# Identity products in TensorE's waits: an eight-layer attention and feed-forward kernel on one core

## What is computed

```python
x = x + L0_xattn(ctx, norm(x))   # causal attention of the 56 tokens over the first 56 context rows
x = x + L0_ffn(norm(x))          # 8 experts, top 2 by softmax gates, gelu
x = x + L1_xattn(norm(x), ctx)   # self attention, cross attention over 1500 keys, two linear maps, three layer norms
x = x + L1_ffn(norm(x))          # gated unit with 4 bit weights and 16 bit activations, five maxima over all of x
x = x + L2_xattn(norm(x), ctx)   # 16 heads of 64, softmax over 1500 keys, output map, layer norm
x = x + L2_ffn(norm(x))          # 64 small units of 16
x = x + L3_xattn(norm(x), ctx)   # 16 heads of 8, masked softmax over 1500 keys
x = x + L3_ffn(norm(x))          # 8 experts, top 2, a layer norm behind each expert
```

## Time and profile before

| | us |
|---|---|
| median of 3 runs | 1704.77 |
| lowest and highest | 1703.37, 1705.45 |
| the profiled execution's own time | 1701.17 |
| its span, first to last instruction | 1699.1 |
| TensorE busy, matmul | 1484.5 |
| VectorE busy | 1248.8 |
| mean granted clock of TensorE | 0.942 |

### The profile page before, as it was taken

One profiled execution on the slowest core, in us unless ns is written; L12 is line 12 of the kernel. 1 busy time (PEld: TensorE's weight loads), 2 busy tenths in 40 slices (PEclk: granted clock), 3 DMA queues, 4 the chain that ended last, 5 costly groups with the idle time before them and its releaser, 6 DMA issues. The chain is left out here.

```text
span 1699.1 us, 39660 instructions
## 1 busy us (share of the span) xinstructions
PE 1484.5 (87%) x15231; PEld 1254.6 (74%) x15231; DVE 1248.8 (74%) x2582; ACT 840.8 (49%) x1266; POOL 331.9 (20%) x447
## 2 busy tenths in 40 slices
PE   3897387447899999999999999969999999996995
PEld 2897255336799999999999998437777777774895
DVE  4312664794788888888888887558888888884698
ACT  1342133133666666666666665245656666552432
POOL 0110000001333333333333330031111110100320
PEclk9899699667999999999999999989999999998998
DMA  1455067100211111111111100045456455531010
GB/s 36 116 168 122 21 158 172 37 1 1 73 37 38 37 36 36 36 36 38 55 44 44 36 0 0 7 105 141 110 122 148 112 129 131 122 85 51 26 38 23
DMA packets 93021, 115.95 MB, mean 68 GB/s; under 512 B 12152, under 2 KB 78248, under 8 KB 92904
## 3 DMA queue, kind: packets, MB, share of 16 engines
q1 hardware_dynamic: 92904, 114.25, 26.3%
HBM read 76.42 MB, written 0.46 MB: 45 GB/s over the span
## 5 line engine op out<-in xcount | busy, mean ns | idle before, releaser
L1643 ACT CAST l2att_PT<-PS 125x512 fp32r<-125x512 f32 x336 | 175.3, 595 | 221.3 <-PE PS L1582 221.3
L2377 DVE TENSOR_REDUCE l3att_parts<-PS 112x1 f32<-112x500 f32 x384 | 245.6, 669 | 50.3 <-PE PS L2115 42.7
L1683 DVE TENSOR_REDUCE l2att_neg<-PS 128x1 f32<-128x1500 f32 x112 | 192.7, 1720 | 77.4 <-PE PS L1575 77.4
L1689 DVE TENSOR_TENSOR l2att_PT<-PS,l2att_PT 125x512 fp32r<-125x512 f32 x336 | 210.1, 681 | 1.5 <-ACT l2att_PT L1643 1.5
L2244 ACT ACTIVATE l3att_P<-PS 125x1344 f32<-125x1344 f32 x128 | 165.2, 1291 | 77.2 <-PE PS L2136 77.2
L1582 PEld LDWEIGHTS PS<-all_ident,l_P 128*125 128x125 f32 x1344 | 163.6, 187 | 14.9 <-DVE l_P L1697 6.3
L1652 ACT ACTIVATE l_P<-PS,l2att_neg 128x1500 f32<-128x1500 f32 x112 | 171.0, 1527 | 3.9 <-DVE l2att_neg L1683 3.9
L1614 PE MATMUL PS<-l2att_PT,l_cc 125*128 125x256 f32 x576 | 170.5, 296 | 0.0
L1582 PE MATMUL PS<-all_ident,l_P 128*125 128x128 f32 x1344 | 165.4, 273 | 4.8 <-DVE l_P L1697 4.8
L1616 PE MATMUL PS<-l2att_PT,l_cc 125*128 125x256 f32 x576 | 162.5, 282 | 0.0
L1618 PE MATMUL PS<-l2att_PT,l_cc 125*128 125x256 f32 x576 | 162.4, 282 | 0.0
(11 more groups left out here) (549 smaller groups left out, 2860.5 us busy)
## 6 DMA issues: line engine op xcount, KB each, us to landing
l3att_KS<-l3att_kh SPq DMA_DIRECT2D x128, 187.5 KB, 4.0
l_cT<-in_ctxT SPq DMA_DIRECT2D x18, 750.0 KB, 6.5
l_c<-in_ctx SPq DMA_DIRECT2D x16, 750.0 KB
l3att_cT<-in_ctxT SPq DMA_DIRECT2D x16, 750.0 KB, 4.4
l3att_KS<-l3att_kl SPq DMA_DIRECT2D x64, 187.5 KB, 4.4
l_QP<-in_ctx SPq DMA_DIRECT2D x10, 672.0 KB
l_QP<-in_ctxT SPq DMA_DIRECT2D x8, 750.0 KB, 7.1
l0f_w<-in_L_ffn_W SPq DMA_DIRECT2D x16, 256.0 KB, 3.1
```

The lines of the kernel that those rows point to most:

```text
L1643: act.copy(PT[:, 4 * g:4 * g + 4, PLACE[u1], 0, :], PS[0:CHUNK, 3 * s1 + g, :].rearrange("k (c r) -> k c r", r=128)).then_inc(hi_in, 1)
L1683: v.tensor_reduce(neg[:, s:s + 1], E, XY_AXES, ALU.max, negate=True).then_inc(top_in, 1)
L1689: v.tensor_tensor(PT[:, 4 * g:4 * g + 4, at, 1, :], PS[0:CHUNK, 3 * s1 + g, :].rearrange("k (c r) -> k c r", r=128), PT[:, 4 * g:4 * g + 4 ...
L2377: v.tensor_reduce(parts[:, u % 2, half, i:i + 1], PS[0:HROWS, PLACES[p], 0:BANK_KEYS], X_AXIS, ALU.max, negate=True).then_inc(top_in, 1)
```

## The change

A helper `keep_busy(pe, bank, count)` multiplies the 128 x 128 identity by itself `count` times into a given bank, whose content nothing uses. Each product is two weight loads and two matmuls. It is called 18 times in one execution, 474 products in all, unrolled: in `l0a` 5, 14 and 30; in `l0f` 28; in `l1s` 30, 14, 52 and 44; in `l1c` 40 and 46; in `l1q` 20, 30, 18 and 14; in `l2fold` 30; in `l2m` 22; in `l3att` 7; in `l3f` 30. The counts are fixed. The products wait for nothing, and the next real instruction of TensorE stands behind them in its list. In `l1q` the wait for `b_in` also moves ahead of `spread(OQ)`, since the bank that it guards is now written earlier.

```diff
@@ -132,6 +132,11 @@
 
+    def keep_busy(self, pe, bank, count):
+
+        for _ in range(count):
+            pe.matmul(self.PS[:, bank, 0:128], self.ident[:, :], self.ident[:, :], start=True, stop=True)
+
     def sb(self, ctx, name, shape, dt=F32):
@@ -291,9 +296,12 @@
             def _(pe):
+                self.keep_busy(pe, 6, 30 if self_keys else 5)
                 pe.wait_ge(w_in, 80 if self_keys else 32)
...
                           start=True, stop=True).then_inc(fold_ps, 1)
+                if not self_keys:
+                    self.keep_busy(pe, 6, 14)
                 for k in range(2):
@@ -315,9 +323,11 @@
                 if self_keys:
+                    self.keep_busy(pe, 7, 14)
                     pe.wait_ge(cnt_in, 1)
...
                               stop=True).then_inc(len_ps, 1)
+                self.keep_busy(pe, 7, 52 if self_keys else 30)
                 pe.wait_ge(p_done, 1)
@@ -335,6 +345,8 @@
                     mm.then_inc(z_ps, 1)
+                if self_keys:
+                    self.keep_busy(pe, 7, 44)
 
@@ -496,6 +508,7 @@
             def _(pe):
+                self.keep_busy(pe, 6, 30 if final else 28)
                 pe.wait_ge(w_in, 16 * SETUP_DMAS)
@@ -878,6 +891,7 @@
                     mm.then_inc(z_ps, 1)
+                self.keep_busy(pe, 0, 40)
                 pe.wait_ge(n2_ready, 1)
@@ -893,6 +907,7 @@
                     mm.then_inc(y_ps, 1)
+                self.keep_busy(pe, 2, 46)
 
@@ -1159,9 +1174,11 @@
                     if i == 3:
+                        self.keep_busy(pe, 6, 20)
                         spread(GQ)
...
                 products("wvT", "wo", 0, ORDER[0:2])
+                self.keep_busy(pe, 6, 30)
                 spread(UQ)
@@ -1177,8 +1194,10 @@
                 mm.then_inc(cb_ps, 1)
+                pe.wait_ge(b_in, 8)
+                self.keep_busy(pe, ORDER[2], 18)
                 spread(OQ)
-                pe.wait_ge(b_in, 8)
+                self.keep_busy(pe, ORDER[2], 14)
                 for k in range(2):
@@ -1387,6 +1406,7 @@
             def _(pe):
+                self.keep_busy(pe, 0, 30)
                 for k in range(2):
@@ -1817,6 +1837,7 @@
                 outputs(1)
+                self.keep_busy(pe, 3, 22)
 
@@ -2061,6 +2082,7 @@
                     mm.then_inc(xt_ps, 1)
+                self.keep_busy(pe, 0, 7)
                 pe.wait_ge(w_in, 16)
```

## The result

The kernel after takes 1695.06 us in the median of 14 executions (1691.83 to 1699.46), that of before 1703.78 in the median of 14 (1698.98 to 1710.29). The ratio is 0.9948, with a 95% interval of 0.9938 to 0.9959: about 8.9 us won. Forecast were 12.1, a time of 1692.7 and a range of 1685 to 1702. The profiled execution took 1695.17 with a span of 1693.1.

A forecast was written before the change was run, and what follows sets the result against it. TensorE was taken to lose time at half clock (about 197 us of the span) in short stages behind waits. The steps' terms summed to −12.1 us, from 1704.77 to 1692.7 us, with a range of 1685 to 1702.

The forecast's parts named there:

- Steps 1 to 3, 5 and 6: Runs in `l0a` (−2.0, −1.5), `l0f` (−2.5), and `l1s` behind its head (−1.7, −1.2 us): faster work behind waits.
- Step 7: `l1c`, 40 products in a 10.6 us wait: transposes and products behind at full clock, −2.5 us (−2 to −3).
- Step 4: `l1s` head, 30 products overrunning their wait: 0 if the clock holds, +1.6 us if it falls, taken as +0.8.
- The clock rule: Anywhere on TensorE: clock holds over gaps of 2 us or less, even chance at 2.5, more likely lost at nearly 3.
- Step 8: `l1q`, 20 products before `spread(GQ)`, where there is no wait: paid in full, +4.4 us.
- the rival that called it absorbed: The 20 before `l1q`'s gate-maximum spread cost 0, total 1688.3 us; chance 0.08.
- Step 10: `l1q`, 18 before and 14 behind `spread(OQ)`: +0.4 us overrun, −2.3 from output products at full clock.
- Step 11: `l2fold` head, 30 products: 1 us over the wait, or 2.6, against 3 won behind; −1.5 us (−2.2 to 0).
- Step 12: `l2m` 22 and `l3att` 7: six key products at full clock, 2.7 instead of 5.37 us; −1.5 us (0 to −2.2).
- Step 13: `l3f`, 30 products in an 8.4 us wait, VectorE's gate steps stretched beside GpSimd's biases: −1.0 us (0 to −2.2).
- That the clock doesn't rise for these products: All runs: products mostly of zeros leave the clock at half, runs overrun by 57 us, 1761 or more; chance 0.05.
- Half of the wins stop at another engine: Whole kernel: ScalarE's copies, GpSimd or transfers set the end, half the wins remain, 1701.5 us; chance 0.15.

The follow-up runs named there:

- e6_half: The kernel after with every run at half its length: 1701.44 us, ratio 0.9988 to before.
- e9_shift: `e7_best` without the 18 before `l1q`'s third spread and with 14 products added at the end of `l3att`: 1689.95 us, ratio 0.9932 to before.
- e2_only20: The kernel before plus only the 20 products in front of the spread of the gate maximum in `l1q`: ratio 1.0024, 4.1 us slower.
- e10_best_plus20: `e7_best` with the 20 products before the spread of the gate maximum put back: 1692.54 us, ratio 0.9939 to before.
- e8_clear: `e7_best` also without the 18 and 14 in `l1q`, the 22 in `l2m` and the 7 in `l3att`: 1691.44 us, ratio 0.9935 to before.
- e1_no20: The kernel after without the 20 products in front of the spread of the gate maximum in `l1q`: 1692.09 us, ratio 0.9944 to before.
- e7_best: After without `l1q`'s 20 and 30, `l1c`'s 46, the 30 at `l1s`'s head and in `l3f`, with 25 in `l2fold`: 1688.83 us, ratio 0.9915 to before.
- e11_best_plus_l3f: `e7_best` with the 30 products at the head of `l3f` put back: 1686.44 us, ratio 0.9905 to before.
- e12_best_plus_l1s: `e7_best` with the 30 products at the head of `l1s` put back: 1688.83 us, ratio 0.9917 to before.

## Why the prediction was right, and what it mis-sized

What each stage took against before, mean over profiles with the runs less mean over those without (12 changed kernels, `e6_half` left out, and `e9_shift` in the row of steps 9 and 10; `l1q` ends and `l2fold` begins with the change of block, and only three of the seven in the row of steps 9 and 10 have the 30):

| Steps | Forecast, us | Profiles with, without | With less without, us |
|---|---|---|---|
| 1, 2 (`l0a`) | −3.5 | 10, 2 | −3.5 |
| 3 (`l0f`) | −2.5 | 10, 2 | −3.2 (with: −4.3 to −1.9) |
| 4 (`l1s` head) | +0.8 | 5, 7 | +1.1 (0.2 or 1.4 to 1.9) |
| 5, 6 | −2.9 | 10, 2 | −2.4 |
| 7 (`l1c`, 40) | −2.5 | 10, 2 | −1.8 |
| 8 (the 20) | +4.4 | 4, 8 | +4.1 |
| 9, 10 (`l1q`, 30, 18, 14) | −1.9 | 7, 4 | −1.0 (with: −2.3 to −1.2) |
| 11 (`l2fold`) | −1.5 | 10, 2 | −0.5 (with: −3.4 to +1.0) |
| 12 (`l2m`, `l3att`) | −1.5 | 9, 3 | −0.7 |
| 13 (`l3f`) | −1.0 | 5, 7 | −0.3 |

The right column sums to −8.2 us, against 8.9 measured and 12.1 forecast. Single entries are good to about 1 us, and least sure where only two or three profiles are without. The mechanism held and the sizes were too hopeful: steps 7 and 10 to 13 each miss 0.7 to 1.0 us, and step 3 gave 0.7 more. The range took that in.

**Steps 1 to 3, 5 and 6 hold.** Between VectorE's, ScalarE's and TensorE's turns a faster TensorE turn is time won. The price of 0.222 us held: 5.61 − 1.14 = 4.47 us of wait for 20 products are 0.224 each. Step 7 gave 2.2 us against before in nine of the ten profiles, within its bounds, and 0.7 in that of after, in which the clock was at half again from 299.0 to 302.4 us.

**Step 4 holds in both its cases.** "0 or +1.6" were measured as about 0.2 and 1.4 to 1.9. The clock rule behind it was too sharp: gaps of 2.90 us fell out both ways, and so did the 2.1 us from which the rule was made. Timeline, PE, the twelve transposes behind such a gap in `l1c`, of before and then of after:

```profile
286.05 1.57 PE L848 MATMUL PS<-all_ident,l_P 128*125 128x128 f32 x12 [2.10 <-ACT l_P L920]
```

```profile
274.66 2.55 PE L861 MATMUL PS<-all_ident,l_P 128*125 128x128 f32 x12 [2.09 <-ACT l_P L935]
```

In before the clock stayed up, in after it was at half from 275.1 to 281.9.

**Step 8 holds**, shown by `e2_only20` and by `e10_best_plus20`: a run that stands in no wait is paid in full, and by the rival that called it absorbed `e2_only20` would have had ratio 1.0000.

**Step 10 was mis-sized.** The output products became faster just as said: 2.39 us won in all seven profiles with the 18 and 14, where 2.3 were forecast. But the four without any run in `l1q` also scatter there, from 1.1 won to 0.6 lost, since the clock fell at other moments. And the 18 delay the maximum behind `spread(OQ)`, by 0.05 us in after and 0.7 to 1.25 in the other six, 0.9 in the mean, where I had taken 0.4; in `e8_clear` and `e9_shift`, without them, the delay is 0.0. The 30 of step 9 cost nothing, as forecast: from before `spread(UQ)` to behind `spread(OQ)` `e1_no20`, which has the 30 and the 18, lost 1.24 us, and `e7_best`, which has the 18 alone, 1.12.

**Step 11 was mis-sized** in what stands against its overrun. The run reaches past its wait as priced. Against before, the first token copy of `l2fold` came 0.6 us later behind the block's start in after, 2.0 to 2.2 in the three others with 30 products, where the clock fell, 1.0 to 1.1 in four of the six with 25, and 0.5 earlier in `e8_clear` and `e9_shift`, whose 25 ran at full clock (5.82 us). But what the products behind it give back is 1.5 us (with less without), not 3.

**Step 12 was mis-sized.** The key products are faster, 2.0 us at the third chunk, but 1.2 to 4.0 go again in the head of the loop. Timeline, PE, of after, at the place where the clock fell:

```profile
1132.71 0.48 PE L2137 MATMUL PS<-l3att_KS,l3att_QB 97*112 97x500 f32 x1 [0.20 <-DVE l3att_parts L2399]
1133.36 0.48 PE L2137 MATMUL PS<-l3att_KS,l3att_QB 97*112 97x500 f32 x1 [0.17 <-DVE l3att_kl L2363]
1134.62 0.69 PE L2137 MATMUL PS<-l3att_KS,l3att_QB 97*112 97x500 f32 x2 [0.78 <-DVE l3att_parts L2399]
1135.97 0.54 PE L2168 MATMUL PS<-all_ident,l3att_negs 112*3 112x112 f32 x2 [0.67 <-DVE l3att_negs L2432]
```

No gap is longer than 0.78 us, and the clock is at half from 1135.3. My rule looked at single gaps of 2 us and more, and here none stands. Nor do the short ones settle it: in before the same gaps of 0.78 and 0.68 us stand at this place, and the clock stayed up. It fell near there in the profiles with the 22 and 7 and also in the three without, while before happened to stay up. So this is no price of the two runs; that before stayed up there was luck.

**Step 13 was mis-sized**, by GpSimd's additions as shown under `e11_best_plus_l3f`: 2.5 to 2.7 us won from the block's start to the gate values in four of five profiles (0.5 in `e11_best_plus_l3f`), and 3.3 to 3.7 lost behind them in the same four up to the next additions, of which the stretched steps explain some 2; the seven without it lost 1.2 in the mean further on, so that the ends differ by 0.3.

**The rivals.** That the clock doesn't rise for these products is out (0.975, and 0.977 with transposes). That it falls again in each rest is out for these counts, and is what happened at half of them in `l0a`. "Half of the wins stop at another engine" came true in step 13 alone; what steps 10 to 12 miss went to runs that overran and to the clock.

**Left open.** The loop of `l1c`, which holds no runs, took from 5.0 us less to 1.7 more than before in changed kernels. Where the clock falls there differs from profile to profile; why at that moment, no run tells. `e1_no20`'s missing 1 to 3 us are followed in one profile of each kernel only; whether its other executions lost them at the same places isn't shown.

## What to carry to other kernels

A short stage in which engines take turns behind a wait is worth keeping the clock up for, and the run must reach nearly to the end of its wait: at half the length the whole set won 0.1%, which is not clear of nothing. Before each run, look for the engine that is idle because of TensorE at that place; where there is one, as before the spread of the gate maximum, each product of 0.222 us is paid in full. Where the clock may fall just before the run, count its products at 0.42 us: the 25 and 30 of `l2fold` overran their wait in most profiles and gave back part of what step 10 had won. A win of some us that is made early stays, but one that brings two engines together on the same memory, or moves a stage a little, is easily given back, so judge such runs by on-and-off pairs over several executions and not by one profile.

## What the hardware showed unexpectedly

- The clock fell in a stretch whose longest TensorE gap was 0.78 us, and behind the same gap it fell in one profile and held in another: 2.90 us (after, `e12_best_plus_l1s`), 2.48 (`e7_best`, `e8_clear`) and 2.1 (after, before).
- Transposes of the identity held the clock up as well as products: 0.977 against 0.975.
- A VectorE step of 0.22 us on two inputs took 2.16 and 2.06 us beside GpSimd's additions of 2.36 and 2.38, ending 0.07 to 0.08 after them.
- TensorE's "issue" gaps, 4.5 us in 70, came and went in code that nothing had changed.
